# Low halves of the projection weights made on GpSimd instead of VectorE

## The reference, cut to what matters

```python
def _div_clamp_fp8(x, scale):
    y = jnp.clip(x.astype(jnp.float32) / scale, -FP8_MAX, FP8_MAX)
    return _fp8_roundtrip(y.astype(jnp.bfloat16).astype(jnp.float32))

def _fp8_linear_pertensor(x, wq, w_scale, in_scale):      # in_scale has one value for each of the 512 inputs
    xq = _div_clamp_fp8(x, in_scale)
    return jnp.einsum('bsi,oi->bso', xq * in_scale, wq) * w_scale

q  = _ln(_fp8_linear_pertensor(ln_out, wq, wq_scale, q_in_scale).reshape(b, s, g, hpg, d), qln_w, qln_b)
k  = _ln(_fp8_linear_pertensor(ln_out, wk, wk_scale, k_in_scale).reshape(b, s, g, d), kln_w, kln_b)
v  = _fp8_linear_pertensor(ln_out, wv, wv_scale, v_in_scale).reshape(b, s, g, d)
qx = _ln(_fp8_linear_pertensor(ln_out, wqx, wqx_scale, qx_in_scale).reshape(b, s, g, hpg, d), qxln_w, qxln_b)
core = _gqa(q, k, v)            # 16 query heads in 8 groups of 2, head size 128
xout = _gqa(qx, kx, vx)         # the same queries' shape against the context
```

## Time and profile before

| | |
|---|---|
| time, median of 3 runs | 1785.48 us (1784.53 to 1785.58) |
| the profiled execution | 1783.69 us, of which the span of the trace 1781.8 us |
| PE busy | 1737.0 us, 97% |
| DVE busy | 1405.0 us, 79% |
| ACT busy | 1105.4 us, 62% |
| POOL busy | 273.5 us, 15% |

### The profile page before, as it was taken

The page is one execution under the profiler, slowest core; times in us unless marked ns, Lnnn a source line. Parts: engine busy times, 40 slices in busy tenths (PEclk is TensorE's granted clock), DMA queues, the critical chain, the costliest instruction groups (busy, mean ns, idle before and its releaser), DMA issues.

```text
span 1781.8 us, 31332 instructions
## 1 busy us (share of the span) xinstructions
PE 1737.0 (97%) x10664; PEld 1183.0 (66%) x10664; DVE 1405.0 (79%) x4581; ACT 1105.4 (62%) x2378; POOL 273.5 (15%) x428
## 2 busy tenths in 40 slices
PE   9999999988999999999999999999999999989998
PEld 4454444666777777777777777777777777744554
DVE  1243526589889998898899899899889988879996
ACT  1252515376577667667666667767667665657776
POOL 0000000211111111112121111111111112101111
PEclk9999999999999999999999999999999999999999
DMA  8212200101101120120121012111101012000000
GB/s 284 83 59 83 71 24 26 37 1 49 50 19 32 49 68 19 44 68 26 37 66 38 19 44 68 37 44 54 32 19 44 32 48 97 1 1 19 25 25 30
DMA packets 45596, 83.30 MB, mean 47 GB/s; under 512 B 3584, under 2 KB 22528, under 8 KB 45056
## 3 DMA queue, kind: packets, MB, share of 16 engines
q1 hardware_dynamic: 45440, 81.31, 14.1%
HBM read 69.77 MB, written 10.49 MB: 45 GB/s over the span
## 4 chain that ended last, share of the span: by engine, by line
PE 64%; DVE 20%; issue 9%; ACT 3%; POOL 3%; DMA 1%; POOLq 0%; ACTq 0%; DVEq 0%
PE bank L533 14%; PE bank L596 9%; PE bank L642 8%; PE bank L691 5%; PE bank L620 4%; PE bank L727 3%; PE bank L455 3%; PE bank L493 3%; PE bank L575 2%; PE bank L407 2%; DVE nq L1239 2%; PE bank L434 2%; DVE nmx L1389 2%; DVE bnB L1215 2%; PE bank L569 2%
## 5 line engine op out<-in xcount | busy, mean ns | idle before, releaser
L533 PE MATMUL bank<-wqs,XQ 128*128 128x256 f16 x2048 | 245.6, 273 | 5.5 <-DVE x L1270 5.5
L596 PE MATMUL bank<-prT,KV 128*128 128x256 f32 x1024 | 247.5, 385 | 0.0
L642 PE MATMUL bank<-kT,qT 128*128 128x512 f32 x512 | 240.9, 593 | 0.9 <-issue 0.9
L596 PEld LDWEIGHTS bank<-prT,KV 128*128 128x128 f32 x1024 | 190.9, 192 | 73.2 <-issue 52.1
L533 PEld LDWEIGHTS bank<-wqs,XQ 128*128 128x128 bf16 x2048 | 197.6, 98 | 47.3 <-DVE x L1270 21.0
L1009 ACT ACTIVATE pr<-bank,nmx 128x512 f32<-128x512 f32 x256 | 174.4, 688 | 57.2 <-DVE nmx L1389 55.7
L1558 POOL TENSOR_TENSOR rdev<-gvar,cst 128x7 f32<-128x7 f32 x128 | 192.6, 1505 | 10.0
L1556 POOL TENSOR_TENSOR gvar<-mvB,geps 128x7 f32<-128x7 f32 x128 | 30.7, 240 | 1044.8 <-DVE mvB L1229 1044.8
L1389 DVE TENSOR_REDUCE nmx<-bank 128x1 f32<-128x512 f32 x256 | 167.6, 681 | 9.5 <-PE bank L642 7.1
L691 PE MATMUL bank<-identf,pr 128*128 128x128 f32 x1024 | 151.9, 276 | 18.4 <-DVE pr L1249 14.5
L810 ACT ACTIVATE prT<-bank 128x512 f32<-128x512 f32 x256 | 153.1, 614 | 25.7 <-PE bank L691 25.5
(11 more groups left out here) (179 smaller groups left out, 3097.8 us busy)
## 6 DMA issues: line engine op xcount, KB each, us to landing
wst<-in_wcat SPq DMA_DIRECT2D x21, 512.0 KB, 4.0
nq<-in_wgu SPq DMA_DIRECT2D x16, 512.0 KB, 3.5
wpst<-in_wproj SPq DMA_DIRECT2D x8, 1024.0 KB, 6.4
wa<-in_wgu SPq DMA_DIRECT2D x16, 512.0 KB, 3.7
xT<-in_xT SPq DMA_DIRECT2D x4, 1024.0 KB, 7.7
nq<-in_wdn SPq DMA_DIRECT2D x8, 512.0 KB, 3.5
wkx<-in_wkvx SPq DMA_DIRECT2D x8, 512.0 KB, 4.8
tern_gu<-wa SPq DMA_DIRECT2D x16, 256.0 KB, 2.0
```

What stands on the lines that cost most here:

```text
L533: ins = mm(dst, XQ[:, b, c, k, j * P:(j + 1) * P], w, start=(k == 0 and m == 0), stop=(k == KT - 1 and m == 1))
L596: ins = mm(OB[:, 0:2 * P], KV[:, n % 2, t, P:2 * P], prT[:, st % 2, t, :, :].rearrange("p h s -> p (h s)"), start=(t == 0), stop=(t == ST ...
L642: mm(SB_[h][:], qT[:, h, st * P:(st + 1) * P], kT[:, :], start=True, stop=True).then_inc(s["scores_made"], 1)
```

## The change

The low parts that DVE made inside the pair stage are made by POOL. POOL takes two instructions for each tile where DVE took one: it multiplies the staged weights by `srel` in place, and subtracts the high part from them, with a wait on its own semaphore between the multiplications and the subtractions of a half. A half is made in the step in which ACT makes its high part: it stands behind the step's `deviations` in POOL's program, in steps 2 and 3 of pairs b = 0, 1 and 2, and waits for ACT's `wh_ready`. PE's, ACT's and SP's programs are the same. `split_low` of DVE stays for the three parts of group 0.

```diff
@@ DVE, pair(g, b, first, last) @@
                     if T in XSTAT:
                         x_stats(XSTAT[T])
-                    if b == 2 and not last and st == 3:
-                        split_low(3 * (g + 1) + 2, 0)
-                    if b in (1, 2) and not last and st == 1:
-                        split_low(3 * (g + 1) + b - 1, 1)
                     if st == 0:
                         if T >= 2:
                             accumulate(T - 2, (4 * b - 2) % 16)
-                        if b and not last:
-                            split_low(3 * (g + 1) + b - 1, 1 if b == 3 else 0)
                         dve.wait_ge(s["xs_made"], n + 1)
@@ POOL @@
+            def split_low(part, half):
+                pool.wait_ge(s["wh_ready"], 2 * part + half + 1)
+                for c in WPART[part % 3]:
+                    for k in (2 * half, 2 * half + 1):
+                        own.do(g.tensor_scalar(staged(part, c, k), staged(part, c, k), srel[:, c, k:k + 1], None, ALU.mult))
+                own.sync()
+                for c in WPART[part % 3]:
+                    for k in (2 * half, 2 * half + 1):
+                        wh, wl = split_weights(part // 3, c, k)
+                        ins = g.tensor_tensor(wl, staged(part, c, k), wh, ALU.subtract)
+                ins.then_inc(s["wl_ready"], 1)
+
             def pair(gr, b, first, last):
@@
                     if nxt:
                         deviations(4 * n + 4 + st)
+                    if b < 3 and not last and st >= 2:
+                        split_low(3 * (gr + 1) + b, st - 2)
```

## The result

The changed kernel takes 1789.22 us (median of 12 runs, 1788.39 to 1790.23) against 1785.42 us for the kernel before on the same chips: ratio 1.0021, 95% interval 1.0013 to 1.0029. It is slower by 3.8 us. The direction was forecast and the size was not: 1800 us was predicted, 14 us slower. The profiled execution took 1788.44 us, span 1786.4 us, against 1783.69 and 1781.8 us.

What follows compares the result with a forecast made beforehand. It took the chain scores, `nmx`, exponential, `nq`, `pr`, transposes to bound the start of step 0. 1783.7 - 9.7 + 15.5 + 8.4 = 1797.9 us profiled, with 1.8 us added 1799.7, rounded to 1800; range 1775 to 1822, likeliest case 1790 to 1822.

Steps and rivals of the forecast that it cites:

- What bounds the kernel, and where DVE is on the path: Pair stage: DVE delays cost PE time at the start of step 0; step 3 has 1.03 us to spare.
- The gain: DVE's low parts leave the path at b = 2 to b = 3 and in group 0: 9.7 us, between 7.7 and 11.5.
- 7 x 1.10 = 7.7: Step 3 and step 0 from b = 2 to b = 3: 1.10 us saved in each of seven groups, 7.7 us.
- I take 2: Group 0, partly bounded by DVE: 2 us more gain, from a range of 0 to 3.8 us.
- The fourth rival: The 1.10 us at b = 2 to b = 3 come from elsewhere: gain 2 us, 1807 us in all; no chance of its own.
- POOL's time: New POOL work: 28 halves of Q and QX at 2.3 us, 14 of K and V at 3.0 us, 106 us in all.
- The price: POOL's instructions hold DVE's `kn`, `nq` and `pr` in steps 3 and 0: 15.5 us plus 8.4 us.
- 21 such halves: 15.5 us: Second halves, in step 0: each costs one subtraction, 0.74 us (between 0 and 1.9), as DVE's `nq` and `pr` have no slack.
- So 0.40 us spills over, 21 times: 8.4 us: First halves, in step 3: DVE delayed 0.74 us, 0.17 + 0.17 us absorbed in the next step 0; total between 0 and 22.
- The first rival: DVE goes on as if POOL were idle, so only the gain is left: 1776 us, faster; chance 0.34.
- Full blocking: Every POOL instruction meeting `kn`, `nq` or `pr` holds it for its length: 62 us less 9.7, 1838 us; chance 0.10.
- The deviations and `wl_ready`: POOL's deviations queued behind the new work come in time, and the earlier `wl_ready` loads cost nothing.

Runs made afterwards that it cites:

- zeros: Changed kernel with POOL writing zeros into the low parts instead of multiplying and subtracting; 1775.02 us, 0.9950 of the kernel before.
- kv_only: Changed kernel with only K's and V's low parts on POOL, Q and QX back on DVE; 1780.25 us, 0.9979 of the kernel before.
- q_only: Changed kernel with only Q's and QX's low parts on POOL, K and V back on DVE; 1789.13 us, 1.0028 of the kernel before.
- mult_only: Changed kernel with POOL only multiplying, straight into the low part, the subtraction left out; one execution, span 1780.6 us (kernel before: 1781.8).
- sub_only: Changed kernel with POOL only subtracting, the multiplication left out; one execution, span 1782.6 us (kernel before: 1781.8).
- late_q: Changed kernel with both halves of Q and QX moved to the next pair's step 0, waiting until `pr` is scaled; 1777.39 us, 0.9963 of the kernel before.
- shift_q: Changed kernel with Q's and QX's halves moved behind the deviations of steps 0 and 1 of the next pair; 1790.82 us, 1.0040 of the kernel before.

## Why the prediction was right or wrong, point by point

- **What bounds the kernel, and where DVE is on the path.** Right. The chain scores, `nmx`, `nq`, `pr`, transposes bounds step 0 without slack: the 0.81 us read off it above are the 12.56 - 11.75 us of the step. Step 3 passes DVE's lag on.
- **The gain.** 9.7 us was forecast, "7 x 1.10 = 7.7" and 2 for group 0. Measured with zeros: 6 x 1.25 + 0.9 = 8.4 us by the periods. One step of the reading was wrong though the size held: the halves of Q and QX in steps 0 and 1 were taken to cost nothing, and by kv_only and q_only they made the 0.34 us of step 3 of b = 2, and 0.13 us in step 3 of b = 1 (7.94 to 7.81), which the seven did not have. "I take 2" for group 0 was wrong: DVE work was removed there and nothing came of it beyond the usual place. What bounds its long steps was not tried. The fourth rival, that the 1.10 us come from something else, is refuted by 8.14 to 7.80 and 12.51 to 11.75.
- **POOL's time.** Forecast 106 us, measured 163 us with its own waits. The subtraction was put 10% high (0.74 and 0.47 us against 0.67 and 0.42 undisturbed); the multiplication was estimated from a form that has no scalar operand in SBUF for each row, and needs 0.93 us where 0.40 was put (undisturbed, mult_only), 0.60 us on 128 columns.
- **The price, the step that failed.** The prediction puts one subtraction, 0.74 us, on every second half ("21 such halves: 15.5 us") and a spill on every first half ("So 0.40 us spills over, 21 times: 8.4 us"): 1.14 us for each part, three parts alike, 23.9 us in all. Measured over zeros: Q 0.95, QX 0.92, K and V 0.14 us, 2.00 a group, and 0.6 us in group 0: 6 x 2.00 + 0.6 = 12.6 us. Of the 11.3 us too many, 7 are K and V (1.0 us in each of seven groups), 2.5 are Q and QX in six groups (0.41 us each), 1.8 are Q and QX in group 0.
- **Why K and V failed.** They were given the price of Q and QX without a look at which POOL instruction stands beside `pr`. By the prediction's own lengths four multiplications take 4 x 0.29 = 1.2 us, so the subtractions would have begun at 1014.5, still ahead of `pr`; they take 0.60 us each, and the subtractions begin 2.8 to 3.0 us behind the start, when the `pr` that PE waits for is done. So two errors meet here: one price for two orders of instructions, and the multiplication at half its length. sub_only shows the other side, 0.49 us for K and V without the multiplications.
- **Why Q and QX came near, partly by luck.** In the step 0 after b = 0 the spill is 0.35 us where 0.40 was put, but by two errors that cancel: the first half starts behind POOL's deviations, 2.38 us into step 3 and not when ACT releases it, 1.6 us into the step, and so meets both `pr`, and DVE leaves the step 1.0 us late and not 0.74; and the idle time and the back-to-back maxima take up 0.66 us of this and not 0.34. The second half costs 0.16 + 0.29 = 0.45 us on the chain where 0.74 was put. Step 3 itself, put at nothing, costs up to 0.14 us. By the runs with one half alone the split is further off: 0.84 us for the first halves of Q and QX (2 x 0.40 put), 0.38 for the second (2 x 0.74 put), and the rest only where both are there.
- **The sum** with the measured terms: 1783.7 - 8.4 + 12.6 = 1787.9 us, against 1788.44 measured; 0.4 of the missing 0.5 us lie ahead of the first score product (341.03 against 340.60).
- **The first rival, no contention.** Refuted as a whole by `pr` at 0.90 us, true for K and V nearly. The evidence for it, L1258 never held, did not carry over from POOL operands of seven columns: beside operands of 256 columns L1258 took 0.48 us in late_q and once 0.72 us in the changed kernel, against 0.29.
- **Full blocking.** The lock is there, as sub_only shows: DVE ends 0.08 us behind POOL. The rule of the Trainium skill ("SBUF — State Buffer", "Who interferes with whom": the second to issue fully blocks) agrees with that run and with the 0.90 us of `pr`. It does not agree with mult_only, where `kn` passed in the middle of a multiplication. The rival's 62 us did not come. Its upper bounds had every DVE instruction that meets POOL's work held for all that is left of it; in the rows shown one is held to the end of a single POOL instruction, and POOL is held in turn (its two subtractions in step 3 took 1.48 us, in sub_only 1.30). And the back-to-back maxima give 0.26 us of a lag back (1.28 us for two, where they took 1.54 in the earlier trace rows).
- **The deviations and `wl_ready`.** Hidden, as said: the deviations by the numbers under zeros, and no wait of PE for POOL stands among the changed kernel's waits.

## What to carry to other kernels

Before work moves to GpSimd, lay its instructions on the timeline of VectorE and ask which VectorE instruction that some other engine waits for falls beside the two-input ones: the same work cost 0.14 us in one place, 0.95 in another, nothing in a third. A lag on VectorE has to be followed to the next idle time of VectorE itself; slack at the consumer of the delayed instruction is not enough, as shift_q showed. The lengths of the GpSimd instructions decide what stands beside what, so they are worth measuring before the sum is made. A run that keeps order and waits but replaces the disputed instructions by short writes gives gain and price apart in one go.

## What the runs showed of the hardware

- A subtraction of a 128x256 float32 and a float16 tile on GpSimd takes 0.67 us undisturbed, on 128 columns 0.42. VectorE's fast SBUF instructions (0.53 ns a column) that it holds end 0.08 us behind it on 128 columns (`kn`, `nq` in sub_only) and 0.28 us behind it on 512 (`pr` in the changed kernel). That is about their 128 x 0.53 = 0.07 and 512 x 0.53 = 0.27 us, an estimate by which only the reading and writing of the operands waits, and not the start of the instruction.
- A multiplication by a scalar for each row takes 0.93 and 0.60 us, longer than the two-input form, and lets such an instruction through in its middle. Why was not tried.
- Beside GpSimd's writes without reads (zeros of 128x256 and 128x128) `nq` and `pr` kept their lengths (at most 0.35 and 0.49 us) and `kn` took up to 0.45 instead of 0.34. It cost nothing: the steps that held them lasted 7.80 and 11.75 us.
- Group 0 lasted 177.6 us in kv_only's profile, 173.8 in the earlier trace rows. The granted clock of the stretch was 0.94 against 0.97, that is, more time at 1.2 instead of 2.4 GHz; this row is kv_only's:

```profile
340.40:518.00 177.60, 160.94 (x1080) 122.47 (x1091) 149.65 (x500) 114.55 (x258) 39.91 (x58) 0.94 0.11 36
```

  The first two steps alone lasted 27.2 us against 22.6 before. Group 0 went from 172.9 to 177.6 us over the twelve profiles, so spans of single executions can differ by some 5 us without a cause in the edit, and the periods of the later groups were the measure to trust.
